# Mamba, FFN, attention and MoE in one kernel on one core: the state loop steps through pairs of states

## What is computed

```python
def step(h, inp):
    dA, dBx, c = inp
    h = dA * h + dBx
    y = jnp.einsum('ben,bn->be', h, c)
    return (h, y)
# delta = softplus(dt @ dtw + dtb);  A = -exp(A_log)
# deltaA = exp(delta[..., None] * A)
# deltaBx = delta[..., None] * Bm[:, :, None, :] * u[..., None]
# y = scan(...) + Dp * u;  y = y * silu(z);  out = y @ out_w
```

## Time and profile before

| | us |
|---|---|
| median of 3 runs (lowest to highest) | 2601.8 (2599.41 to 2604.18) |
| the profiled execution | 2601.99 |
| its span, first to last instruction | 2600.2 |
| PE busy | 2394.5 (92%) |
| DVE busy | 1860.6 (72%) |
| ACT busy | 1552.6 (60%) |
| POOL busy | 1367.7 (53%) |
| mean granted TensorE clock | 0.968 |
| first Mamba matmul (L735) to last L723 | 74 to 2206 |
| tail without Mamba | about 394 |

### The profile page before, as it was taken

How to read it: one execution, slowest core, us unless ns; L and a number is a source line. 1 busy time by engine, 2 the same in 40 slices (tenths; PEclk the granted TensorE clock), 3 DMA queues, 4 the chain that set the end, 5 groups by cost and what they waited for, 6 DMA issues and landing times.

```text
span 2600.2 us, 41027 instructions
## 1 busy us (share of the span) xinstructions
PE 2394.5 (92%) x14530; PEld 1710.1 (66%) x14675; DVE 1860.6 (72%) x3817; ACT 1552.6 (60%) x3377; POOL 1367.7 (53%) x1227
## 2 busy tenths in 40 slices
PE   7999997999899889989998989998998989989988
PEld 7888884687566546757566656665575656657675
DVE  5879797859796978789688968797878767412220
ACT  1434435556565548664876568665866695566654
POOL 1467483937384765658373837476565738212101
PEclk9999998999899999999999999999999999989989
DMA  4123130323121223112321222122312412010100
GB/s 153 54 78 112 46 96 33 106 82 98 29 86 41 80 65 100 49 64 75 100 80 34 89 86 87 41 74 74 105 46 66 118 50 82 7 47 1 49 5 5
DMA packets 97643, 175.34 MB, mean 67 GB/s; under 512 B 11957, under 2 KB 23133, under 8 KB 95646
## 3 DMA queue, kind: packets, MB, share of 16 engines
q1 hardware_dynamic: 97438, 172.71, 21.9%
HBM read 157.44 MB, written 15.23 MB: 66 GB/s over the span
## 4 chain that ended last, share of the span: by engine, by line
PE 67%; ACT 13%; DVE 11%; issue 5%; POOL 4%; DMA 0%; POOLq 0%; SPq 0%; ACTq 0%; DVEq 0%
PE c_bank L928 14%; PE c_bank L1359 13%; PE c_bank L920 13%; PE a_bank L766 7%; PE b_bank L1068 3%; DVE hst L714 2%; PE a_bank L756 2%; PE a_bank L735 2%; ACT hid L955 1%; ACT weighted_y L963 1%; POOL prod_c L837 1%; PE b_bank L588 1%; PE b_bank L1058 1%; PE b_bank L1107 1%; PE a_bank L772 1%
## 5 line engine op out<-in xcount | busy, mean ns | idle before, releaser
L837 POOL TENSOR_TENSOR prod_c<-hst,prod_c 128x512 f32<-128x512 f32 x512 | 671.0, 1318 | 326.7 <-DVE hst L714 321.8
L714 DVE TENSOR_TENSOR_SCAN hst<-dA,a_bank 128x512 f32<-128x512 f32 x512 | 620.9, 1213 | 13.5 <-ACT dA L826 3.8
L920 PE MATMUL c_bank<-c_xT,w 128*128 128x512 f32 x1024 | 533.7, 627 | 38.3 <-ACT hid L955 25.2
L928 PEld LDWEIGHTS c_bank<-w,hid 128*128 128x128 f32 x4096 | 501.8, 194 | 71.8 <-ACT hid L955 36.6
L928 PE MATMUL c_bank<-w,hid 128*128 128x128 f32 x4096 | 518.0, 278 | 10.9 <-ACT hid L955 7.6
L1359 PEld LDWEIGHTS c_bank<-ident 128*128 128x128 f32 x3994 | 483.2, 193 | 39.0 <-issue 31.6
L826 ACT ACTIVATE dA<-delta,a_neg 128x510 f32<-128x510 f32 x512 | 365.0, 719 | 229.3 <-DVE hst L714 221.2
L1359 PE MATMUL c_bank<-ident 128*128 128x128 f32 x3994 | 491.5, 276 | 2.2 <-DVE bc L662 0.3
L955 ACT ACTIVATE hid<-c_bank,b 128x512 f32<-128x512 f32 x512 | 348.1, 688 | 144.9 <-PE c_bank L920 143.3
L979 POOL TENSOR_TENSOR xs<-xs,weighted_y 128x512 f32<-128x512 f32 x128 | 167.2, 1306 | 467.2 <-ACT weighted_y L963 466.5
L708 DVE TENSOR_TENSOR a_bank<-du,a_bank 128x512 f32<-128x512 f32 x512 | 348.3, 680 | 35.2 <-PE a_bank L756 24.2
(11 more groups left out here) (177 smaller groups left out, 2801.2 us busy)
## 6 DMA issues: line engine op xcount, KB each, us to landing
prod_c<-c_rows SPq DMA_DIRECT2D x512, 256.0 KB, 3.2
q_and_k<-qk_rows SPq DMA_DIRECT2D x64, 192.0 KB
qk_rows<-att_buf SPq DMA_DIRECT2D x40, 256.0 KB, 2.6
w<-in_w SPq DMA_DIRECT2D x2, 2048.0 KB
xs<-in_x SPq DMA_DIRECT2D x8, 256.0 KB, 6.7
bias<-skew SPq DMA_DIRECT2D x1, 2048.0 KB, 8.4
qk_rows<-b_xn SPq DMA_DIRECT2D x8, 256.0 KB, 2.9
out_dram<-xs SPq DMA_DIRECT2D x8, 256.0 KB, 2.3
```

The lines of the kernel that those rows point to most:

```text
L714: nc.vector.tensor_tensor_scan(hst[:, s % RS, :], dA[:, s % RA, :], b_bank, 0.0, ALU.mult, ALU.add).then_inc(M.h.sem, 1)
L837: nc.gpsimd.tensor_tensor(prod[:, s % RP, :], hst[:, s % RS, :], cring[:, s % RC, :], ALU.mult).then_inc(M.pp.sem, 1)
L920: nc.tensor.matmul(S.bank[up_bank(e, c)][:, :], w1[:, e, c * 128:(c + 1) * 128], S.xT[:, :], start=True, stop=True).then_inc(M.up.sem, 1)
L928: ins = nc.tensor.matmul(S.bank[down_bank(f)][:, t * D:(t + 1) * D], hid[:, f % 2, j, t * 128:(t + 1) * 128], w2[:, f, j, :], start=(j == ...
```

## The change

The loop goes over `PAIRS` = 16 pairs of states a pass instead of 32 steps.

- Banks 1 and 2 of lane a become one PSUM tensor `two` of 128x2x512. PE writes both B rows of a pair into it with two matmuls, the second of which signals. The pair's matmuls wait for the scan of the pair just before (`M.h` at p), since there is no second set of banks. The sums of the products go to bank 0.
- DVE does one product and one scan over 1024 columns for a pair. `RA` and `RS` become 4, that is two pairs each. ACT still makes one decay for each state, and waits once for two.
- POOL does one product of state and C over 1024 columns for a pair, then the same addition of 512 columns as before.
- SP brings two C rows with one DMA: 256 DMAs of twice the bytes instead of 512.
- In the softplus the maximum with zero is taken earlier, before the logarithm is awaited (`M.tm`), so banks 0 and 1 are free when the loop begins, and two DVE operations are left in `softplus_end` in place of three. The first pair's B rows wait for it.
- `drT` and `bcC` share one buffer, which makes room for the longer rings.
- All five order tables are new. The count of L1359 matmuls in PE's goes from 1997 to 1807.

```diff
--- before.py
+++ after.py
...
 PT = 6
-RS, RA, RP, RC = 3, 3, 4, 4
+RS, RA, RP, RC = 4, 4, 4, 4
+PAIRS = STEPS // 2
...
 ORDER_PE = (
-    "b2d9bd45bd4b2d6b2d6b2d29bd4b3d39b5dbd57adbdaba2bd4b2d3ad6b2ad4a2d10ad13bd13adb2d3bd2ad7ad30a2d11ad15a2d7ad3"
...
+    "b2d8bd37bd3b2d5b2d6b2d28bd3b3d38b6d57aba3b2d9b2ad5ab2a2d29ad14bd6ad20b3d2a2d15a2d12a2d26a2d27b3a2b3d4a2b3da2"
...
                 self.shift = sb(f"{s}_shift", [128, TT])
-                self.bank = [ctx.enter_context(nc.psum_tensor(f"{s}_bank{i}", [128, 512], F32)) for i in range(banks)]
+                first = ctx.enter_context(nc.psum_tensor(f"{s}_bank0", [128, 512], F32))
+                if s == "a":
+                    self.two = ctx.enter_context(nc.psum_tensor("a_bank1_2", [128, 2, 512], F32))
+                    self.bank = [first, self.two[:, 0, :], self.two[:, 1, :]]
+                else:
+                    self.bank = [first] + [ctx.enter_context(nc.psum_tensor(f"{s}_bank{i}", [128, 512], F32)) for i in range(1, banks)]
...
         sz = sb("sz", [128, HALVES, TOK])
-        drT = sb("drT", [RANK + 1, TOK])
-        bcC = sb("bcC", [128, TOK])
+        low_high = sb("dt_rank_and_c", [128, TOK])
+        drT, bcC = low_high[0:RANK + 1, :], low_high[:, :]
         bch = sb("bch", [128, TOK], BF16)
...
         s_wc = plain("moe_weights_loaded")
-        s_c = [plain(f"c_row_loaded_{i}") for i in range(RC)]
+        s_c = [plain(f"c_rows_loaded_{i}") for i in range(RC // 2)]
         s_cst = plain("c_rows_in_dram")
...
                 self.delta = sig(n + "_delta", 2, use, uses)
-                self.b = sig(n + "_b_row", STEPS, use, uses)
+                self.b = sig(n + "_b_row_pair", PAIRS, use, uses)
                 self.dA = sig(n + "_decay", STEPS, use, uses)
-                self.dBx = sig(n + "_dbx", STEPS, use, uses)
-                self.h = sig(n + "_state", STEPS, use, uses)
-                self.pp = sig(n + "_product", STEPS, use, uses)
-                self.pair = sig(n + "_product_pair", STEPS // 2, use, uses)
+                self.dBx = sig(n + "_dbx_pair", PAIRS, use, uses)
+                self.h = sig(n + "_state_pair", PAIRS, use, uses)
+                self.pp = sig(n + "_product_pair", PAIRS, use, uses)
+                self.pair = sig(n + "_product_pair_added", PAIRS, use, uses)
+                self.tm = sig(n + "_softplus_max", 2, use, uses)
                 self.sum = sig(n + "_state_sum", STEPS // 2, use, uses)
...
+            for h in range(HALVES):
+                dve.wait_ge(L.sem, step[h])
+                nc.vector.scalar_tensor_tensor(out=delta[:, h, :], in0=S.bank[h][:, :], scalar=0.0, in1=delta[:, h, :],
+                                               op0=ALU.max, op1=ALU.subtract).then_inc(M.tm.sem, 1)
+                yield
             duh = [0, 0]
...
                 dve.wait_ge(M.l.sem, L.at(M.l, h + 1))
-                dve.wait_ge(L.sem, step[h])
-                nc.vector.tensor_tensor(xc[:, h, :], xc[:, h, :], delta[:, h, :], ALU.subtract).then_inc(L.sem, L.one())
-                yield
-                dve.wait_ge(L.sem, L.n)
-                nc.vector.scalar_tensor_tensor(out=delta[:, h, :], in0=S.bank[h][:, :], scalar=0.0, in1=xc[:, h, :],
-                                               op0=ALU.max, op1=ALU.add).then_inc(M.delta.sem, 1)
+                dve.wait_ge(M.tm.sem, L.at(M.tm, h + 1))
+                nc.vector.tensor_tensor(delta[:, h, :], delta[:, h, :], xc[:, h, :], ALU.add).then_inc(M.delta.sem, 1)
...
                 nc.vector.scalar_tensor_tensor(out=yT[:, h, :], in0=u[:, h, :], scalar=chan[:, 1, l, h:h + 1],
-                                               in1=S.bank[1][:, :], op0=ALU.mult, op1=ALU.add).then_inc(M.yD.sem, 1)
+                                               in1=S.bank[0][:, :], op0=ALU.mult, op1=ALU.add).then_inc(M.yD.sem, 1)
...
             yield from softplus_end(0)
-            for s in range(STEPS):
-                h, n = s // NST, s % NST
-                dve.wait_ge(M.b.sem, L.at(M.b, s + 1))
+            two = S.two[:, :, :]
+            for p in range(PAIRS):
+                h, n = 2 * p // NST, 2 * p % NST
+                r = p % 2 * 2
+                state = hst[:, r:r + 2, :]
+                dve.wait_ge(M.b.sem, L.at(M.b, p + 1))
                 if n == 0:
                     dve.wait_ge(L.sem, duh[h])
-                b_bank = S.bank[2 - s % 2 * 2][:, :]
-                nc.vector.tensor_tensor(b_bank, du[:, h, :], b_bank, ALU.mult).then_inc(M.dBx.sem, 1)
-                yield
-                dve.wait_ge(M.dBx.sem, L.at(M.dBx, s + 1))
-                dve.wait_ge(M.dA.sem, L.at(M.dA, s + 1))
-                if s >= RS:
-                    dve.wait_ge(M.pp.sem, L.at(M.pp, s - RS + 1))
-                nc.vector.tensor_tensor_scan(hst[:, s % RS, :], dA[:, s % RA, :], b_bank, 0.0,
+                nc.vector.tensor_tensor(two, du[:, h, :].unsqueeze(1).to_broadcast([128, 2, TOK]), two, ALU.mult).then_inc(M.dBx.sem, 1)
+                yield
+                dve.wait_ge(M.dBx.sem, L.at(M.dBx, p + 1))
+                dve.wait_ge(M.dA.sem, L.at(M.dA, 2 * p + 2))
+                if p >= 2:
+                    dve.wait_ge(M.pp.sem, L.at(M.pp, p - 1))
+                nc.vector.tensor_tensor_scan(flat(state), flat(dA[:, r:r + 2, :]), flat(two), 0.0,
                                              ALU.mult, ALU.add).then_inc(M.h.sem, 1)
...
-                if s == 1:
+                if p == 0:
                     yield from softplus_end(1)
-                if s == NST + 3:
+                if p == NST // 2 + 1:
                     yield from half_end(0)
...
             pe.wait_ge(M.bcS.sem, L.at(M.bcS, 1))
-            for s in range(STEPS + 4):
-                if s < STEPS:
-                    if s == 1:
-                        pe.wait_ge(M.delta.sem, L.at(M.delta, 1))
-                    elif s:
-                        pe.wait_ge(M.h.sem, L.at(M.h, s - 1))
-                    nc.tensor.matmul(S.bank[2 - s % 2 * 2][:, :], sel[:, s % NST, :], bc3[:, :],
-                                     start=True, stop=True).then_inc(M.b.sem, 1)
-                    yield
-                if s >= 4 and s % 2 == 0:
-                    k = s // 2 - 2
+            for p in range(PAIRS + 2):
+                if p < PAIRS:
+                    if p == 0:
+                        pe.wait_ge(M.tm.sem, L.at(M.tm, 2))
+                    else:
+                        pe.wait_ge(M.h.sem, L.at(M.h, p))
+                    for i in range(2):
+                        ins = nc.tensor.matmul(S.bank[1 + i][:, :], sel[:, (2 * p + i) % NST, :], bc3[:, :], start=True, stop=True)
+                    ins.then_inc(M.b.sem, 1)
+                    yield
+                if p >= 2:
+                    k = p - 2
                     pe.wait_ge(M.pair.sem, L.at(M.pair, k + 1))
...
                         pe.wait_ge(M.yD.sem, L.at(M.yD, 1))
-                    nc.tensor.matmul(S.bank[1][:, :], ident[:, :], prod[:, 2 * k % RP, :],
+                    nc.tensor.matmul(S.bank[0][:, :], ident[:, :], prod[:, 2 * k % RP, :],
                                      start=(k % (NST // 2) == 0), stop=(k % (NST // 2) == NST // 2 - 1)).then_inc(M.sum.sem, 1)
...
                     act.wait_ge(M.delta.sem, L.at(M.delta, h + 1))
-                if s >= RA:
-                    act.wait_ge(M.h.sem, L.at(M.h, s - RA + 1))
+                if s >= RA and s % 2 == 0:
+                    act.wait_ge(M.h.sem, L.at(M.h, s // 2 - 1))
                 nc.scalar.activation(half_batches(dA[:, s % RA, :], 1), half_batches(delta[:, h, :], 1), ACT.Exp,
...
             yield from rstd_pool(pool, L, S, M.norm.stats, M.norm.rstd, rms=True)
-            for s in range(STEPS):
-                pool.wait_ge(s_c[s % RC], 16 * (i * STEPS // RC + s // RC + 1))
-                if s >= RP:
-                    pool.wait_ge(M.sum.sem, L.at(M.sum, s // 2 - 1))
-                pool.wait_ge(M.h.sem, L.at(M.h, s + 1))
-                nc.gpsimd.tensor_tensor(prod[:, s % RP, :], hst[:, s % RS, :], cring[:, s % RC, :],
-                                        ALU.mult).then_inc(M.pp.sem, 1)
-                yield
-                if s % 2:
-                    pool.wait_ge(M.pp.sem, L.at(M.pp, s + 1))
-                    nc.gpsimd.tensor_tensor(prod[:, (s - 1) % RP, :], prod[:, (s - 1) % RP, :], prod[:, s % RP, :],
-                                            ALU.add).then_inc(M.pair.sem, 1)
-                    yield
+            for p in range(PAIRS):
+                r = p % 2 * 2
+                pool.wait_ge(s_c[p % 2], 16 * (i * PAIRS // 2 + p // 2 + 1))
+                if p >= 2:
+                    pool.wait_ge(M.sum.sem, L.at(M.sum, p - 1))
+                pool.wait_ge(M.h.sem, L.at(M.h, p + 1))
+                nc.gpsimd.tensor_tensor(prod[:, r:r + 2, :], hst[:, r:r + 2, :], cring[:, r:r + 2, :], ALU.mult).then_inc(M.pp.sem, 1)
+                yield
```

(13 more changed lines are left out.)

130 lines of the change are left out of this document (60 added, 70 removed).

## The result

The change takes 2706.4 us (median of 4 runs, 2703.4 to 2710.0) against 2602.8 (2599.4 to 2604.2), a ratio of 1.040 with an interval of 1.0386 to 1.041. The forecast was 2580 with a range up to 2618. The profiled execution spans 2701.6 us, 101.4 more than before. In this and all later figures two executions of over 4700 us are left out, one of e3 and one of the kernel before that ran beside e1 to e4.

What follows compares the result with a forecast made beforehand. The prediction took DVE and PE, both nearly full in the 16 Mamba passes, to bound the kernel. From a base of about 2602 us, -43 + 15 - 11 + 10 + 10 - 3 = -22 gave 2580 us, range 2552 to 2618.

Steps and rivals of the forecast that it cites:

- The tally: Work on DVE and PE between B rows, longer side taken, over 16 loops: 1379 us against 1422, so -43 us.
- Step 1: Longer DVE products and scans in the state loop: -56 us of DVE work, bounds nothing to -75.
- Step 2: B rows no longer run ahead: 0.8 us at each of 240 places, 57 of 192 us uncovered on DVE.
- The mark I had set: Sign for the handshake: DVE's total wait for B rows over 100 us, where near 60 was expected.
- Step 3 and 4: Work moved out of the loops, +15 us; at the loop's ends, -11 before the first product and +10 after the last scan.
- the +10: End of the loop: POOL can start only when both scans are done, 16 x 0.6 us.
- The -11 for the early maximum: Start of the loop: one DVE operation of 0.69 us less between logarithm and first product, 16 x 0.7 us.
- Step 5: POOL's longer products hold up DVE operations in SBUF: +40 us of DVE time, a quarter showing, +10.
- Step 6: C rows' paired DMAs and the tail: nothing for the C rows, -3 us for the tail.
- The handshake eats it: Rival, 2620 us: late B rows and scans stall DVE and PE, +42 us on top of the tally; chance 0.14.
- No change: Rival, 2602 us: work moved out of the loops costs 31 us and POOL's hold-up of DVE 20; chance 0.14.

Runs made afterwards that it cites:

- e3: The change with POOL's C product split into two of 512 and DVE's products, scans and B-row handover done row by row; 2708.0 us, ratio 1.039.
- e1: The change with POOL's 1024-wide product of state and C issued as two instructions of 512; 2691.5 us, ratio 1.034.
- e4: The kernel before with POOL's C product done once over 1024 columns for two steps; 2664.8 us, ratio 1.024.
- e2: The change with DVE's product and scan as two of 512 and each B row waiting only for its own bank's scan; 2719.5 us, ratio 1.045.
- e10: The change in the kernel before's queue order, pair's sum behind the next B rows, all instructions 512 wide, B rows released bank by bank; 2754.6 us, ratio 1.057.
- e9: The change in the kernel before's queue order, but with a pair's sum on PE behind the next B rows; 2758.3 us, ratio 1.060.
- e8: The kernel before with only the softplus maximum taken early, ahead of the logarithm; 2611.9 us, ratio 1.003.
- e6: The change with POOL's C product cut to 16 columns a row in all passes but the first; 2656.4 us, ratio 1.020.
- e7: The kernel before with POOL's C products cut to 16 columns in all passes but the first; 2586.6 us, ratio 0.993.
- e16: The kernel before with both C products of two steps behind the second scan, as two instructions of 512; 2641.4 us, ratio 1.014.
- e12: The change with the input product scanned in place in SBUF, freeing banks early, and POOL's C product cut to 16 columns; 2697.3 us, ratio 1.036.
- e15: The change with the input product scanned in place in SBUF, freeing banks early, and POOL's product and sum cut short; 2678.6 us, ratio 1.028.
- e17: e15 with 140 of the 240 pairs of B rows moved earlier in PE's queue; 2667.9 us, ratio 1.025.

## Why the prediction was wrong

- **The tally** is the step that failed. It gave 1379 us for the loops and the trace has 1511. It summed what stands on DVE and on PE between two B rows and took the longer side, as if each queue ran without waits of its own and PE at one speed. That it met before's trace within 5 us (1422 against 1416.7 in the cut used here, where the prediction has 1427) was no proof for the change: in before a row stands ready while the scan runs, and in the change none does. Waits in PE's view grew by 93 us, the work on PE took some 50 us longer, and no term of the sum was for either.
- **Step 1** was right in size: 2.28 and 1.22 us, 72 us less of records, 56 forecast in spacing. Its worth was less: going back to 512 columns with the handover row by row costs 13 us (e2) to 17 (e3 against e1). With POOL's product narrowed too nothing of it is left: e3 and the change are 2 us apart, e10 and e9 4.
- **Step 2** was right where nothing else runs: 4.25 us a pair in the second pass, as forecast, and its loop 9 us longer (4 to 6 forecast, the rest is two held-up operations). It was wrong elsewhere. I counted only DVE's uncovered time and wrote that it costs nothing where PE is the longer side. PE's queue is the nearly full one, and behind each wait for a scan there stands the MoE, and behind that ACT, POOL and the FFN, where most of the 93 us appeared. The mark I had set, over 100 us of DVE waiting, was met (103).
- **Step 3 and 4**: the stretches between the loops grew by 23 us in all, 14 forecast. The epilogues' share of +12.6 is near the +10. The -11 for the early maximum isn't there; e8 shows +8.
- **Step 5** had the mechanism and missed the size. I averaged over random meetings and let a quarter of 40 us show. The meetings are systematic, since filler and POOL's product mostly start at the same scan's end. The pairs e6 and e7 give 32 us, and 15 of them are had back by e1. The late start of the even state's product had no term at all; it costs 37 us in the kernel before (e16), but in the change, where the sum stands behind the rows, PE waits only 5.6 us for it (8.6 before), so its price there isn't shown.
- **Step 6**: the C rows landed in time (3.6 us against the 5.0 there is), and the nothing for it was right but for three waits of POOL, 17.7 us in all. The tail was 17 us shorter, 3 forecast; PE is busy for 15.6 us less in it, which fits with work moved into the longer Mamba stage.
- **The clock.** PE ran at 1.2 GHz for 93 us more, and its work took some 50 us longer, which ate the 42 us of the dropped matmuls. I had left it out. Whether it adds to the loss or only follows from PE's waits wasn't separated: no run changed the one without the other.
- **The rivals.** "The handshake eats it" had the right side and the right kind of reason, with +42 us on top of the tally, less than half of what came. I gave it 0.14 because its direct rows were small. The direct rows stayed small: 24 of the 93 us. The rest is other waits, most of them behind these as I read the ledger. The sum of "No change" was off: 31 for 15 and 20 for 10 make 2606, not 2602.

What stays open: how the 72 us without POOL divide between the missing slack, the work bunched in twos, the clock and this particular order. That the missing slack is the larger part is argued, not shown: the runs that freed a bank earlier (e2, e3, e12, e15) gained nothing, and e17, which also moved 140 of the pairs of rows, regained 8 us. Whether a better order or other places for the unread matmuls regain more than the 52 of 154 us no run here tells.

## What to carry over

Where two nearly full in-order queues meet at every step, meeting in twos cost far more (151 us in e10) than the longer instructions it allowed were worth (13 to 17). Count who stands behind each wait on the fuller engine, since a tally of work alone can meet the old trace and still miss the new one. Freeing the buffer earlier doesn't help as long as the place in the queue stays. When a change makes an engine wait for two results in place of one, price the late start of the first as well. And check what a longer POOL instruction starts together with, because work on DVE that fills the same gap meets it most of the time. Where filler work is taken from PE, look whether the granted clock falls with it.

## What the runs showed of the hardware

- DVE operations with all operands in SBUF can wait out POOL's instruction, up to its whole 2.4 us (a 0.69 us operation took 2.41, one of 704 columns 2.93 in place of 0.89). A scan with both inputs in SBUF does so too (4.38 us in place of 2.28), and POOL's sum in turn waits for the scan (3.14 us in place of 1.3). A scan that reads one input from PSUM doesn't stretch (2287 ns is the longest of 256 in the change).
- An instruction over two adjacent PSUM banks costs no more than its columns: scan 2280 ns for 1024 against 1213 for 512.
- With waits added and filler matmuls removed, PE gained no busy time from the removal: with POOL out, 2390.4 us at a granted clock of 0.969 against 2392.3 at 0.957 with 190 matmuls less.
